# A gated cross-attention block: first norm from a transposed copy of x, token centres on ScalarE, last down product by halves

## The reference

```
# x, ctx: 16 batches x 256 tokens x 512
q = layernorm(x)                                   # 8 heads of 64
gates = [q, ctx, ctx] @ igate / fgate + bias       # per token and head
log_D = (cumsum of log_sigmoid(fg), row - column) + ig, lower triangle
D = exp(log_D - row maximum)
C = (q @ ctx.T / 8) * D
h = C / (max(|row sum of C|, exp(-maximum)) + 1e-6) @ ctx, RMS-normed per head
x = x + tanh(g_xattn) * h
t = layernorm(x)                                   # then a feed-forward part
g, u = int8(t) @ ternary(w_gate).T, int8(t) @ ternary(w_up).T     # 2048 wide
y = int8(relu(g)**2 * u) @ ternary(w_down).T       # scale of int8: maximum of the row
x = x + tanh(g_ffn) * y
```

## Time and profile before

| | |
|---|---|
| median of 3 runs | 602.35 us (601.4 to 603.7) |
| profiled execution | 605.11 us, its span 603.4 us |
| mean granted TensorE clock | 0.986 |
| TensorE busy | 578.3 us, 96% |
| VectorE busy | 526.2 us, 87% |
| ScalarE busy | 453.1 us, 75% |
| GpSimd busy | 129.9 us, 22% |
| DMA | 62.68 MB, mean 104 GB/s |
| chain that ended last | TensorE 81%, ScalarE 8%, VectorE 5%, issue 4% |

### The profile page before, as it was taken

How to read it: one execution, slowest core, us unless ns; L and a number is a source line. 1 busy time by engine, 2 the same in 40 slices (tenths; PEclk the granted TensorE clock), 3 DMA queues, 4 the chain that set the end, 5 groups by cost and what they waited for, 6 DMA issues and landing times.

```text
span 603.4 us, 18384 instructions
## 1 busy us (share of the span) xinstructions
PE 578.3 (96%) x6571; PEld 339.0 (56%) x6571; DVE 526.2 (87%) x1150; ACT 453.1 (75%) x926; POOL 129.9 (22%) x284
## 2 busy tenths in 40 slices
PE   7986779999999999999999999999999999999996
PEld 3744435656565655656565655656565655655452
DVE  3799897998989898998989898998989898997964
ACT  4799888686876868686886869687786868687661
POOL 3267142120311212120211213120221213120100
PEclk9999879999999999999999999999999999999998
DMA  9959050050605023050504023050504114020100
GB/s 315 382 194 316 28 174 21 23 189 4 211 0 190 20 92 117 18 192 0 210 0 172 37 77 132 18 192 0 197 12 143 66 43 168 20 89 1 37 18 35
DMA packets 44114, 62.68 MB, mean 104 GB/s; under 512 B 1849, under 2 KB 25649, under 8 KB 44081
## 3 DMA queue, kind: packets, MB, share of 16 engines
q1 hardware_dynamic: 44080, 62.24, 29.6%
HBM read 53.72 MB, written 8.51 MB: 103 GB/s over the span
## 4 chain that ended last, share of the span: by engine, by line
PE 81%; ACT 8%; DVE 5%; issue 4%; POOL 1%; DMA 1%; SPq 0%; DVEq 0%; ACTq 0%; POOLq 0%
PE yb L1230 17%; PE gb L1204 17%; PE ub L1204 16%; PE tp L1251 8%; PE ab L1238 7%; PE ab L1218 4%; PE tp L1278 3%; PE ab L1261 3%; PE ab L1239 2%; ACT wdT L528 1%; ACT wgT L536 1%; POOL stage L446 1%; PE ab L1312 1%; DVE stage L810 1%; DMA xs<-in_x 1%
## 5 line engine op out<-in xcount | busy, mean ns | idle before, releaser
L1204 PE MATMUL gb<-wgT,xqT 128*128 128x512 bf16 x512 | 133.6, 384 | 0.0
L1204 PE MATMUL ub<-wuT,xqT 128*128 128x512 bf16 x512 | 132.6, 382 | 0.5 <-DVE stage L810 0.3
L1230 PE MATMUL yb<-wdT,stage 128*128 128x512 bf16 x512 | 124.0, 387 | 4.2 <-ACT stage L558 4.2
L544 ACT ACTIVATE relu<-gb 128x512 f32<-128x512 f32 x128 | 75.3, 588 | 45.9 <-PE gb L1204 45.5
L810 DVE TENSOR_TENSOR stage<-relu,ub 128x512 f32<-128x512 f32 x128 | 86.9, 679 | 16.2 <-ACT relu L546 16.2
L1204 PEld LDWEIGHTS ub<-wuT,xqT 128*128 128x128 bf16 x512 | 49.5, 98 | 63.5 <-DVE stage L810 4.8
L546 ACT ACTIVATE relu<-relu 128x512 f32<-128x512 f32 x128 | 80.8, 631 | 4.1
L937 DVE SCALAR_TENSOR_TENSOR dmat<-ab,dmat 128x384 f32<-128x384 f32 x128 | 65.1, 550 | 19.3 <-POOL dmat L454 13.3
L1230 PEld LDWEIGHTS yb<-wdT,stage 128*128 128x128 bf16 x512 | 47.8, 99 | 54.6 <-issue 5.0
L1204 PEld LDWEIGHTS gb<-wgT,xqT 128*128 128x128 bf16 x512 | 46.1, 101 | 45.4 <-issue 1.9
L454 POOL TENSOR_SCALAR_AFFINE_SELECT dmat<-dmat 128x256 f32<-128x256 f32 x128 | 55.7, 463 | 59.5 <-ACT dmat L604 46.8
(11 more groups left out here) (131 smaller groups left out, 893.7 us busy)
## 6 DMA issues: line engine op xcount, KB each, us to landing
dmat<-max_rows SPq DMA_DIRECT2D x15, 1024.0 KB, 5.1
values<-in_ctx_v SPq DMA_DIRECT2D x16, 520.0 KB, 7.6
xs<-in_x SPq DMA_DIRECT2D x16, 512.0 KB, 5.9
cT<-in_ctx_t SPq DMA_DIRECT2D x16, 512.0 KB, 6.9
out<-stage SPq DMA_DIRECT2D x32, 256.0 KB, 2.0
stage<-in_w_gate SPq DMA_DIRECT2D x4, 1024.0 KB, 12.1
stage<-in_w_up SPq DMA_DIRECT2D x4, 1024.0 KB, 13.5
stage<-in_w_down SPq DMA_DIRECT2D x4, 1024.0 KB, 7.1
```

The lines of the kernel that those rows point to most:

```text
L544: nc.scalar.activation(relu[:, c % 2, :], gb[c % 2][:, :], ACT.Relu).then_inc(g_free, 1)
L1204: last = nc.tensor.matmul(bank[c % 2][:, :], xqT[par][:, t, d, :], w[:, d, c * CH:(c + 1) * CH], start=(d == 0), stop=(d == KD - 1))
L1230: done = nc.tensor.matmul(yb[:, :], hqT[:, c, :], wdT[:, c, :], start=(c == 0), stop=(c == KF - 1))
```

## The change

The host lays a second copy of x beside the first, transposed by batch (`x_t`), and SyncE loads it into `qT` directly, one more DMA of 512 KB per batch from batch 2 on. `attention_norm`, `q_columns` and `columns` remain for batches 0 and 1 alone. For the others TensorE's `stat_rows` turns the two means and the two reciprocal roots, each read as a column repeated 128 times, into rows that stand on all partitions of `yb`; VectorE's `norm_rows` subtracts and multiplies `qT` by them in place; `down(b - 1, 1)`, which writes `yb` next, waits for both halves of that.

The centres of the second norm move from VectorE to ScalarE, in front of `tokens_rstd`, with their sign turned (and turned back by -127 in the scale); VectorE keeps the maxima and takes `hidden(b, 1, 1)` ahead of them. In the last step the maximum is split after two chunks, not three, and its first piece stands earlier. At the end VectorE copies the first half of the columns and ScalarE the second, `down` of the last half is done as two products of 256 columns in two banks, and output and store follow by halves. Eight warming matmuls are added in the prologue.

```diff
@@ -358,10 +364,14 @@
+            def turned(n, par):
+                sp.dma_start(qT[par][:, :, :], x_t[bass.ds(n, 1), :, :].rearrange("o (k p) s -> p (o k) s", p=P)).then_inc(xt_in[par], 16)
+
             def load(n, par):
...
                 queries(n, par)
+                turned(n, par)
                 keys(n, par)
@@ -405,9 +415,12 @@
             schedule(sp, step)
-            store(LAST, 1)
+            for e in range(2):
+                cols = slice(D // 2 * e, D // 2 * (e + 1))
+                sp.wait_ge(o_ready, 2 * B + e)
+                sp.dma_start(out[LAST:B, P:S, cols].rearrange("o p d -> p (o d)"), ot[1][:, cols]).then_inc(out_done[1], 16)
             for t in range(T):
-                sp.wait_ge(out_done[t], 16 * B)
+                sp.wait_ge(out_done[t], 16 * (B + t))
@@ -635,12 +648,19 @@
+            def token_centres(n, npar):
+
+                act.wait_ge(ln2_step, LN2_K * n + 4)
+                for t in range(T):
+                    nc.scalar.activation(xm[:, t, :], x2[npar][:, t, :], ACT.Identity, scale=-1.0,
+                                         bias=mv2[:, t, 0:1]).then_inc(centred, 1)
+
             def tokens_rstd(n):
...
             def quantise_second(n):
-                act.wait_ge(ln2_step, LN2_K * n + 12)
+                act.wait_ge(ln2_step, LN2_K * n + 10)
                 nc.scalar.activation(xq[:, 1, :], xm[:, 1, :], ACT.Copy, scale=qs[:, 1:2], bias=MAGIC16).then_inc(xq_ready, 1)
@@ -673,6 +693,7 @@
             magnitudes(1, 2, 4)
+            token_centres(0, 0)
             tokens_rstd(0)
@@ -728,9 +749,6 @@
                     squares(n)
-                if m is not None:
-                    for t in range(T):
-                        columns(m, qT[par], t)
                 quantise_high(b, 0)
@@ -748,6 +766,7 @@
                 if n is not None:
+                    token_centres(n, npar)
                     tokens_rstd(n)
@@ -766,7 +785,10 @@
             quantise_high(LAST, 1)
-            hidden_cols(LAST, 1)
+            act.wait_ge(y_full, 2 * LAST + 1)
+            act.wait_ge(a_full[1], hidden_use(LAST, 1) + 1)
+            nc.scalar.activation(hqT[:, KF // 2:KF, :], abh[1].rearrange("p (k s) -> p k s", s=P), ACT.Copy,
+                                 bias=-MAGIC16).then_inc(a_free[1], 1)
@@ -810,16 +832,16 @@
-            def hidden_max(b, t, part):
+            def hidden_max(b, t, part, chunks=NC - 1):
...
                 if part == 0:
-                    dve.wait_ge(h_done, 8 * b + 4 * t + 3)
-                    nc.vector.tensor_reduce(h[t][:, FF:FF + 1], h[t][:, 0:3 * CH], axis=AX_X, op=ALU.max,
+                    dve.wait_ge(h_done, 8 * b + 4 * t + chunks)
+                    nc.vector.tensor_reduce(h[t][:, FF:FF + 1], h[t][:, 0:chunks * CH], axis=AX_X, op=ALU.max,
                                             apply_absolute_value=True).then_inc(quant_step, 1)
...
                     dve.wait_ge(quant_step, QUANT_K * (2 * b + t) + 1)
-                    nc.vector.tensor_reduce(hmax[:, t:t + 1], h[t][:, 3 * CH:FF + 1], axis=AX_X, op=ALU.max,
+                    nc.vector.tensor_reduce(hmax[:, t:t + 1], h[t][:, chunks * CH:FF + 1], axis=AX_X, op=ALU.max,
                                             apply_absolute_value=True).then_inc(quant_step, 1)
@@ -883,6 +905,19 @@
+            def norm_rows(m, par):
+
+                dve.wait_ge(rows_full, m - 1)
+                dve.wait_ge(xt_in[par], turned_loads(m, par))
+                halves = [qT[par][:, :, t * P:(t + 1) * P] for t in range(T)]
+                for t in range(T):
+                    mean_row = yb[:, None, t * P:(t + 1) * P].to_broadcast([P, KD, P])
+                    nc.vector.tensor_tensor(halves[t], halves[t], mean_row, ALU.subtract).then_inc(q_step, 1)
+                for t in range(T):
+                    rstd_row = yb[:, None, S + t * P:S + (t + 1) * P].to_broadcast([P, KD, P])
+                    dve.wait_ge(q_step, 2 * m - 3 + t)
+                    nc.vector.tensor_tensor(halves[t], halves[t], rstd_row, ALU.mult).then_inc(q_ready, 1)
+
             def gates_in(m):
@@ -997,30 +1032,27 @@
-            def token_centres(n, npar):
+            def token_maxima(n):
                 k = LN2_K * n
                 for t in range(T):
-                    dve.wait_ge(ln2_step, k + 3 + t)
-                    nc.vector.tensor_scalar(xm[:, t, :], x2[npar][:, t, :], mv2[:, t, 0:1], None, ALU.subtract).then_inc(ln2_step, 1)
-                for t in range(T):
-                    dve.wait_ge(ln2_step, k + 5 + t)
+                    dve.wait_ge(centred, T * n + t + 1)
                     nc.vector.tensor_reduce(amax[:, t:t + 1], xm[:, t, :], axis=AX_X, op=ALU.max,
...
                 k = LN2_K * n
...
-                nc.vector.scalar_tensor_tensor(qs[:, :], rstd2[:, :], 127.0, ram[:, :], ALU.mult, ALU.mult).then_inc(ln2_step, 1)
+                nc.vector.scalar_tensor_tensor(qs[:, :], rstd2[:, :], -127.0, ram[:, :], ALU.mult, ALU.mult).then_inc(ln2_step, 1)
@@ -1057,7 +1089,7 @@
             running_max(1, 1)
-            token_centres(0, 0)
+            token_maxima(0)
             quantise_tokens(0)
@@ -1100,7 +1132,7 @@
                 if m is not None:
-                    attention_norm(m, par)
+                    norm_rows(m, par)
                 hidden_max(b, 0, 0)
@@ -1148,21 +1180,27 @@
                     hidden(b, 1, 0)
-                if n is not None:
-                    token_centres(n, npar)
+                if prev:
+                    hidden(b, 1, 1)
+                if n is not None:
+                    token_maxima(n)
                 if not prev:
                     scale_weight(2, 3)
-                else:
-                    hidden(b, 1, 1)
                 if n is not None:
                     quantise_tokens(n)
+                if n is None:
+                    hidden_max(b, 1, 0, NC // 2)
                 hidden_cols(b, 0)
...
                     negated_max(m)
-                hidden_max(b, 1, 0)
+                if n is not None:
+                    hidden_max(b, 1, 0)
                 hidden(b, 1, 3)
-                hidden_max(b, 1, 1)
+                if n is not None:
+                    hidden_max(b, 1, 1)
+                else:
+                    hidden_max(b, 1, 1, NC // 2)
                 if n is not None:
@@ -1171,8 +1209,18 @@
             schedule(dve, step)
-            hidden_cols(LAST, 1)
-            output(LAST, 1, LAST % 2)
+            dve.wait_ge(a_full[0], hidden_use(LAST, 1) + 1)
+            dve.wait_ge(y_full, 2 * LAST + 1)
+            nc.vector.tensor_scalar(hqT[:, 0:KF // 2, :], abh[0].rearrange("p (k s) -> p k s", s=P), MAGIC16, None,
+                                    ALU.subtract).then_inc(a_free[0], 1)
+            for e, bank in enumerate((yb, gb[0])):
+                cols = slice(D // 2 * e, D // 2 * (e + 1))
+                dve.wait_ge(y_full, 2 * B + e)
+                if e == 0:
+                    dve.wait_ge(dq_ready, 2 * B)
+                    dve.wait_ge(out_done[1], 16 * LAST)
+                nc.vector.scalar_tensor_tensor(ot[1][:, cols], bank[:, cols], dq[:, 1:2], x2[LAST % 2][:, 1, cols],
+                                               ALU.mult, ALU.add).then_inc(o_ready, 1)
@@ -1218,11 +1266,13 @@
-            def down(b, t, first, last):
+            def down(b, t, first, last, m=None):
...
                         pe.wait_ge(o_ready, 2 * b + t)
+                    if c == 0 and m is not None:
+                        pe.wait_ge(q_ready, Q_K * (m + 1))
                     if c % (KF // 2) == 0:
@@ -1261,6 +1311,19 @@
+            def stat_rows(b, m):
+
+                pe.wait_ge(rstd_step, RSTD_K * (m + 1))
+                pe.wait_ge(stat_step, STAT_K * (m + 1))
+                if at(b, 0):
+                    pe.wait_ge(winv_step, WSUM[1])
+                else:
+                    pe.wait_ge(o_ready, 2 * b - 1)
+                alone(pe, pe_passed)
+                for i, stat in enumerate((mv[:, 0, 0:1], mv[:, 1, 0:1], rstd[:, 0:1], rstd[:, 1:2])):
+                    last = nc.tensor.transpose(yb[:, i * P:(i + 1) * P], stat.to_broadcast([P, P]), ident[:, :])
+                last.then_inc(rows_full, 1)
+
             def gate_products(m, par, first, last, tiles=GATE_TILES):
@@ -1270,8 +1333,10 @@
                             pe.wait_ge(ct_in[par], loads_of(m, par))
+                        elif at(m, 0, 1):
+                            pe.wait_ge(a_free[t], column_use(m) + 1)
                         else:
-                            pe.wait_ge(a_free[t], column_use(m) + 1)
+                            pe.wait_ge(q_ready, Q_K * m + t + 1)
                     src, row = (cT[par], KD + kd) if part == 0 else (qT[par], kd)
@@ -1372,7 +1437,7 @@
             max_columns(1)
-            keep_warm(6, ub[1])
+            keep_warm(14, ub[1])
             weight_total(1)
@@ -1397,6 +1462,8 @@
                     scores(n, 7, npar)
+                if m is not None:
```

(44 more changed lines are left out.)

6 lines of the change are left out of this document (3 added, 3 removed).

## The result

The changed kernel takes 643.66 us (median of 4 runs, 641.75 to 645.19), the kernel before 603.03 us beside it: ratio 1.0674, 95% interval 1.0647 to 1.0701. It is slower by 6.7%. The forecast was 631.4 with a range of 615 to 643. The sign and the mechanism held, the size did not, and the time lies 0.7 us outside the range.

What follows compares the result with a forecast made beforehand. The prediction took TensorE's work (34.16 us) to bound, with the three-engine loop just behind; lengthened to 36.41, the loop adds 2.25 in 13 steps: 29.2 + 3.65 - 0.6 - 3.2 = +29.0 on 602.35, 631.4 us, range 615 to 643.

Steps and rivals of the forecast that it cites:

- What bounds the kernel: Regular step: TensorE's own work 34.16 us; a loop of waits through TensorE, ScalarE and VectorE 33.82, only 0.34 shorter.
- TensorE's edits: TensorE, each step: loses `q_columns`, 1.23 us, gains `stat_rows`, 0.62; net -0.61.
- Norm on VectorE: VectorE's stretch without pause: four operations, 2.44 us, replace two of 0.91; +1.53 per step, bounds +1.1 and +2.1.
- the two shorter paths: Regular step by the gate path (log of the forget gate) 35.4 us, by the bank of chunk 2 35.7.
- Centres on ScalarE: ScalarE, ahead of the logarithm and L558: two centres delay L558 by 1.06 us, bounds 0.9 and 1.3.
- The clock: TensorE before the cumulative sum: a 1.8 us wait per step, with no fall of the clock behind it in the sum.
- the clock's case: Rival: clock falls behind the 1.8 us wait in half the steps or more, +7 to +20 us, about 641; chance 0.15.
- The base: Starting time for the sum: median 602.35 us, 2.8 below the profiled execution's 605.1; +29.0 was added to the median.
- Start: Prologue and step 0: centres +1.06, then +1.53 and +1.06 in the chain before `down(0, 0)`; together +3.65 us.
- Step 14 and the end: Step 14 -0.6 us from centres off VectorE; end -3.2: earlier scale 1.3, clock staying up 1.6, shorter output 0.3.
- DMA: One more 512 KB load per step, landing in 5.9 us, wanted some 20 us later: costs nothing.
- The rivals: TensorE bound, about 590 (0.07); clock falls, about 641 (0.15); smaller cost, 614 (0.13); table load, above 660 (0.02).

## Why the prediction was right and wrong

*What bounds the kernel.* Right. That 3 us of idle VectorE is not slack, and that the loop through the three engines is only 0.34 us shorter than TensorE's work, was the step that gave the sign. The loop, with the norm at its measured price and the centres, is 36.45, forecast 36.41.

*TensorE's edits.* Right: `stat_rows` runs from 329.11 until the next chunk at 329.81, 0.70 with a hand-over in it, forecast 0.62.

*Norm on VectorE.* 2.39, forecast 2.44; alone it gives 35.55, inside the 35.4 to 35.7 of the two shorter paths.

*Centres on ScalarE.* Mis-sized: 1.23 a pair, forecast 1.06. The figure in the Trainium skill (VectorE: DVE Perf Modes, "The TRN2 errata") that I set aside was exact: 0.61 each. The row that I took, the squares, has the same size and memories, but another function and no column operand. Yet the whole loop came out at 36.45 and not 0.17 above 36.41. The centres alone also cost less than their price: 34.98, where 33.82 + 1.23 would be 35.05. My loop was read 0.1 too long somewhere; no run shows where. Nor does a run tell which of the two differences makes the squares quicker.

*The clock.* This is the step that failed: the sum priced the new 1.8 us wait as a wait alone and put the fall of the clock behind it at nothing. The forecast had it as a rival, at 7 to 20 us and a chance of 0.15. It took 9.4 of the 39.16: ten of thirteen steps at 0.95. The evidence for it was in the rows: falls in the stretches with waits of 3.43 us and of 1.35 and 0.82, and the earlier trace rows, and no regular step with any wait at all. The trace has waits without a fall too, which the rows don't show: 1.15 and 1.27 us in the prologue, before 67.66 and 75.06, with the clock at 1.00 from 66 to 80 us. A forecast that puts a wait of 1.8 us in each of thirteen steps should have given the clock's case far more than 0.15. With 0.95 for ten steps it would have read 640.9.

*The base.* This is a smaller failure. Of the 12.3 us by which the forecast is short, the terms read from the profiles account for 8.2. The rest, 4.1, is the 2.8 by which the profiled execution before lies above the median that I added them to, and the 1.3 by which the profiled execution after lies below its own. My sum took 1.6 us off for a fall of the clock at the end that this execution had the earlier trace rows and the median need not have. Two other profiled executions measure what it had too much: step 1 begins at 91.42 in place of 92.60 in the kernel with the new end alone, whose code is the same up to there, and the end takes 32.80 in place of 34.50 in the kernel with the centres alone. Together that is 2.9. That the median lacks both is inferred from the sum. The fast executions before weren't profiled.

*The range.* It took in half of the clock's case on top of the forecast, and stopped at 643. The upper end of that case (+20) would have held.

*Start.* +1.96, forecast +3.65. The two terms were about right: `down(0, 0)` starts at 87.06 in place of 84.27, +2.79. But before, that product had run at the low clock, 3.60 us. Now TensorE waited less directly ahead of it, 1.94 in place of 3.43, and it ran at full clock. The clock was low earlier instead (0.52 from 76 to 80 us):

```profile
87.06 1.90 PE L1280 MATMUL yb<-wdT,stage 128*128 128x512 bf16 x7 [1.94 <-ACT stage L571]
```

I had priced the same effect at the end (1.6 us) and forgotten it here. But the row below is from the kernel with the new end alone, where nothing has changed up to this product, and there it ran at full clock too, so the 1.7 us belong to the profiled execution and not to the change. Against that run the start grew by 3.14 (94.56 in place of 91.42), near the 3.65.

```profile
83.56 1.90 PE L1252 MATMUL yb<-wdT,stage 128*128 128x512 bf16 x8 [2.75 <-ACT stage L561]
```

*Step 14 and the end.* -3.92, forecast -3.8. The step is 31.60 in place of 32.15, the two waits are 0.65 and 0.43 (forecast 0.65 and 0.4), the clock stayed up, the last output took 0.48. That the number agrees is in part luck: both sides count the fall of the clock in the one profiled execution before. Against an end without it (32.80) the stretch lost 2.2.

*DMA.* Right, nothing; the loads of keys and values behind it land in 7.9 and 8.5 us, and no wait for one of them is among the long ones.

*The rivals.* The eight warming matmuls, which the forecast put at nothing, decide in the kernel with the norm alone between 678 and 640 us, by where they put the loop. The changed kernel without them wasn't tried. I costed what the matmuls do, and not where they move the code.

## What to carry to other kernels

Price a new wait of TensorE twice: the wait itself, and the product behind it at half clock, less what a later wait hides of that. In a loop that is bound elsewhere, filling the wait with idle products can be faster than leaving it empty. And read the waits for issue and the packets of the instruction queue before believing that an edit is slow: a loop whose instructions are loaded anew in each turn may only need to be moved. And before subtracting a fall of the clock that one profiled execution shows, ask whether the median has it at all.

## What the runs showed of the hardware

The clock fell in ten of thirteen steps behind a wait of 1.73 to 1.76 us, and didn't in three with 1.75 to 1.80. In the two other kernels that keep this wait and load their loop once it was ten of thirteen as well. It stayed up in all thirteen steps with the wait filled (0.29 us or less left, and another of 1.43 in the second), and in all thirteen of the centres alone (waits up to 0.83 us). What decides between a fall and none at the same wait is open. A fall costs 1.7 us of products.

A loop of TensorE's instructions, 817 matmuls and weight loads a step and two steps a turn, was either loaded once (20 packets, 0.33 MB) or again and again (65 packets, 1.06 MB), and then cost two waits a turn, of 4.1 to 4.6 and 1.7 to 2.3 us, and a lower clock behind that. Four matmuls ahead of the loop decided between 641.6 and 595.7 us. The packets are 16.3 KB, as the Trainium skill has it (Runtime: NRT & Kernel Launch, "Instruction fetch mechanics": blocks of 16 KiB, and a taken branch to a block outside those held stalls). Its sentence that only two blocks are held doesn't fit the 20 packets of a loop of over 1,600 instructions; the 2,048 instructions that it gives for this engine would: by an estimate from its 256 instructions a block these are eight blocks. The 45 packets more are nine for each of the five jumps back of a loop of six turns. A turn that touches nine blocks would be loaded whole each time, one that touches eight never, and which it is would depend on where the loop starts in a block. That nine blocks come in each turn of the two slow kernels, and none in the middle of the loop of the eleven others, the packets show; that eight are held is argued from it, not shown.

GpSimd took 1.24 us for a tensor by row operation of 512 fp32 elements with a repeated operand, twice VectorE's 0.60, which read that operand from PSUM and not from SBUF.
